# Down products of three feed-forward blocks with stationary weights over 512 tokens, copied by ScalarE and turned back behind the next middle product

## What is computed

```python
def _tlin(x, w, s):
    return jnp.einsum('bsi,oi->bso', x, w) * s
h = silu(_tlin(xn, w1_w, w1_s)) * _tlin(xn, w2_w, w2_s)     # 128 -> 512 features ("up")
h = gelu(_tlin(h, h1_w, h1_s))                              # 512 -> 512 (first middle product)
h = gelu(_tlin(h, h2_w, h2_s))                              # 512 -> 512 (second middle product)
ffn = _tlin(h, w3_w, w3_s)                                  # 512 -> 128 ("down")
# the state-space part: y of 256 features per token, gated, and then projected to 128
attn = residual + jnp.einsum('bli,di->bld', y * silu(z), out_proj_w)
x = x + attn + ffn                                          # both are added to the same rows
```

## Time and profile before

| what | value |
| --- | --- |
| median of three timed runs | 603.2 us (603.0 to 603.21) |
| the profiled execution, its own time | 603.02 us |
| span of its trace, first to last instruction | 600.9 us |
| mean granted TensorE clock | 0.994 |
| busy share of the span: PE, DVE, ACT, POOL | 94%, 66%, 78%, 20% |

### The profile page before, as it was taken

One profiled execution on the slowest core, in us unless ns is written; L12 is line 12 of the kernel. 1 busy time (PEld: TensorE's weight loads), 2 busy tenths in 40 slices (PEclk: granted clock), 3 DMA queues, 4 the chain that ended last, 5 costly groups with the idle time before them and its releaser, 6 DMA issues.

```text
span 600.9 us, 11244 instructions
## 1 busy us (share of the span) xinstructions
PE 562.0 (94%) x3944; PEld 330.8 (55%) x3944; DVE 399.1 (66%) x1060; ACT 470.0 (78%) x669; POOL 120.8 (20%) x161
## 2 busy tenths in 40 slices
PE   6899999999999999999887899698699999999998
PEld 3343434443443434333334587386478887887887
DVE  6784887666363453685527355887888788698773
ACT  5699999989899999999795366479598686685673
POOL 2063221120020030103601355112012010010010
PEclk9999999999999999999999999999999999999999
DMA  7212011024222210400317220200000000000000
GB/s 223 47 25 67 2 27 47 11 88 159 89 107 107 89 72 2 137 6 14 112 42 227 66 77 37 83 2 0 1 1 2 1 17 1 2 17 1 2 19 17
DMA packets 30982, 30.72 MB, mean 51 GB/s; under 512 B 6848, under 2 KB 20960, under 8 KB 30928
## 3 DMA queue, kind: packets, MB, share of 16 engines
q1 hardware_dynamic: 29680, 27.45, 14.6%
q0 software_dynamic: 1248, 2.57, 1.2%
HBM read 13.44 MB, written 12.89 MB: 44 GB/s over the span
## 4 chain that ended last, share of the span: by engine, by line
PE 70%; DVE 15%; ACT 7%; issue 6%; DMA 1%; POOL 0%; DVEq 0%; ACTq 0%; another core or an unknown queue 0%; POOLq 0%
PE ps L1414 18%; PE ps L1393 9%; PE ps L92 6%; PE ps L94 6%; PE ps L93 5%; ACT r L1002 3%; PE ps L1725 2%; PE ps L1494 2%; PE ps L1600 1%; PE ps L1307 1%; PE ps L1763 1%; PE ps L1766 1%; PE ps L1486 1%; PE ps L1730 1%; PE ps L1267 1%
## 5 line engine op out<-in xcount | busy, mean ns | idle before, releaser
L1002 ACT ACTIVATE r<-ps 128x1024 f32<-128x1024 f32 x272 | 257.5, 1041 | 19.6 <-PE ps L1393 17.0
L1414 PE MATMUL ps<-r 128*32 128x512 f32 (+3 forms) x1280 | 144.8, 539 | 0.9 <-DVE r L2185 0.5
L858 POOL TENSOR_SCALAR_AFFINE_SELECT r<-r 128x512 f32<-128x512 f32 (+1 forms) x80 | 47.0, 589 | 206.0 <-ACT r L1002 205.7
L1393 PE MATMUL ps<-r2r 32*128 32x512 f32 (+3 forms) x640 | 80.2, 445 | 4.2 <-ACT r L1002 2.5
L1393 PEld LDWEIGHTS ps<-r2r 32*128 32x128 f32 x640 | 35.6, 182 | 46.9 <-ACT r L1002 21.3
L901 POOL TENSOR_TENSOR r<-r 128x512 f32<-128x512 f32 x16 | 22.6, 1414 | 151.0 <-ACT r L1210 130.1
L1414 PEld LDWEIGHTS ps<-r 128*32 128x32 f32 x1280 | 27.7, 108 | 40.5 <-issue 27.3
L94 PE MATMUL ps<-r2r 128*128 128x512 f32 (+1 forms) x104 | 39.0, 375 | 0.0
L1279 PE MATMUL ps<-consts 128*128 128x512 bf16 x98 | 25.4, 400 | 8.4 <-DMA consts<-in_consts 4.4
L93 PE MATMUL ps<-r2r 128*128 128x512 f32 (+1 forms) x88 | 32.7, 372 | 0.0
L876 POOL DMA_INDIRECT rows_by_token<-r x23 | 23.6, 1025 | 23.8 <-ACT r L1065 14.1
(11 more groups left out here) (436 smaller groups left out, 1206.6 us busy)
## 6 DMA issues: line engine op xcount, KB each, us to landing
rows_by_expert<-r SPq DMA_DIRECT2D x34, 258.0 KB, 2.5
r2r<-r2r SPq DMA_DIRECT2D x56, 64.0 KB, 2.0
r<-in_f_W SPq DMA_DIRECT2D x1, 2048.0 KB, 9.4
r<-rows_by_expert SPq DMA_DIRECT2D x23, 64.5 KB, 1.8
res<-in_x SPq DMA_DIRECT2D x4, 256.0 KB, 4.0
r<-in_g_h1T SPq DMA_DIRECT2D x1, 1024.0 KB
r<-in_g_h2T SPq DMA_DIRECT2D x1, 1024.0 KB
r<-rows_by_token SPq DMA_DIRECT2D x4, 256.0 KB, 4.0
```

What stands on the lines that cost most here:

```text
L858: pool.affine_select(blk, blk, pattern, ALU.is_ge, nothing, base=0, channel_multiplier=-1).then_inc(s_msk, 1)
L1002: act.activation(probs[:, n % PBUFS, :, :], ps[:, b:b + 2, :], ACT.Exp).then_inc(s_exp, 1)
L1393: m = pe.matmul(ps[:, 2 * (n % SBUFS) + h, at:at + TB - query], kst[32 * j:32 * j + 32, group, P * kt:P * kt + P], qst[32 * j:32 * j + 32, ...
L1414: m = pe.matmul(ps[32 * j:32 * j + 32, 6, query:TB], vp[:, kt, group, :], probs[:, (2 * v + j // 2) % PBUFS, j % 2, at:at + TB - query], s ...
```

## The change

`down(b)` of blocks 0 to 2 swaps the operands. The weights `f3[:, k, :]` are now stationary and the activations `fc[k]` of all 512 tokens move: four matmuls of 512 columns, and two of 384 columns with the projection weights `owT` stationary for the first three tiles. The result has features on partitions. ScalarE copies it into SBUF (`down_copied`, in slot 0 of the next block, ahead of its first Gelu). TensorE turns it back with four 128x128 transposes (`turned_back`) behind the first middle product of the next block, into a PSUM bank that it now takes in the round as a unit "BACK". VectorE's `down_added(b - 1)` moves from the end of slot 0 to slot 2, between `state_carried` and `last_chunk_added`. Block 3 keeps the old form under the name `last_down`.

What waited for `s_f4` because the activations or `yg` were still being read waits for the new `s_fdt` (the new down product) instead. The middle product that reuses the bank of the down product waits for the copy (`s_fdc`), and the first of the second middle products waits for `down_added` through the bank of the turned result. To free two semaphores, two counters are merged into others, `s_skt` into `s_kt` and `s_pace` into `s_msk`; the same instructions wait for the same events.

```diff
+        down_features = xn_flat[:, TB:2 * TB]
...
         for b in range(NB):
-            FFN_PE += [("MID1", b, o) for o in range(FO)]
+            for o in range(FO):
+                FFN_PE += [("MID1", b, o)] + ([("BACK", b - 1, 0)] if b and not o else [])
...
             def last_gelu(b, o):
                 act.wait_ge(s_f3, FO * b + o + 1)
                 if b:
-                    act.wait_ge(s_f4, b)
+                    act.wait_ge(s_fdt, b)
...
+            def down_copied(b):
+                act.wait_ge(s_fdt, b + 1)
+                act.activation(down_features, ps[:, ffn_bank("DOWN", b, 0), :], ACT.Copy).then_inc(s_fdc, 1)
...
                         gated_high(b, FO - 1)
                         if not b:
                             decays(0)
+                        else:
+                            down_copied(b - 1)
                     middle_gelu(b, o)
...
             def down(b):
                 bank_free(("DOWN", b, 0))
+                own = TPB - 1
+                for k in range(FO):
+                    pe.wait_ge(s_fg3, FO * b + k + 1)
+                    pe.matmul(ps[:, ffn_bank("DOWN", b, 0), :], f3[:, k, :], fc[k], start=(k == 0), stop=False)
+                pe.wait_ge(s_cg, TPB * b + own)
+                for m_ in range(MI):
+                    m = pe.matmul(ps[:, ffn_bank("DOWN", b, 0), 0:P * own].rearrange("p (n t) -> p n t", n=own),
+                                  owT[:, m_, :], yg[:, 0:own, m_, :], start=False, stop=(m_ == MI - 1))
+                m.then_inc(s_fdt, 1)
+
+            def turned_back(b):
+                bank_free(("BACK", b, 0))
+                pe.wait_ge(s_fdc, b + 1)
+                for i in range(TPB):
+                    m = pe.transpose(ps[:, ffn_bank("BACK", b, 0), P * i:P * i + P], down_features[:, P * i:P * i + P],
+                                     ident)
+                m.then_inc(s_f4, 1)
...
                 for o in range(FO):
                     middle(b, o)
+                    if b and not o:
+                        turned_back(b - 1)
...
-                down(b)
+                if b < NB - 1:
+                    down(b)
+                else:
+                    last_down(b)
...
                         state_carried(s // 2 - 1)
                         if o == 2 and b:
+                            down_added(b - 1)
                             last_chunk_added(b - 1)
                             finished(b - 1)
                         weighted(s // 2)
-                        if o == 0:
-                            down_added(b - 1)
```

More of the change, by code:

```diff
@@ L386, in build @@
         s_ksplit = sem("key_splits_ready")
-        s_kt = sem("first_keys_and_queries_transposed")
+        s_kt = sem("first_keys_and_queries_turned_and_spread")
         s_kc = sem("transposed_keys_copied")
         s_sqc = sem("first_query_stacks_copied")
-        s_skt = sem("first_key_stacks_spread")
         s_skc = sem("first_key_stacks_copied_by_act")
@@ L397, in build @@
         s_vws = sem("summary_values_compact")
-        s_msk = sem("diagonals_masked")
+        s_msk = sem("diagonals_masked_then_late_rows_moved")
         s_og = sem("gated")
@@ L429, in build @@
         s_scat = sem("rows_scattered")
-        s_pace = sem("rows_moved_by_gpsimd")
         s_hs = [sem(f"slot_rows_loaded{g}") for g in range(NG)]
@@ L492, in build @@
         s_f4 = sem("ffn_down_products")
+        s_fdt = sem("ffn_down_features")
+        s_fdc = sem("ffn_down_features_copied")
         s_fr = sem("ffn_scaled")
@@ L870, in _ @@
                 rows_scattered(i)
-                pool.sem_inc(s_pace, 1)
+                pool.sem_inc(s_msk, 1)
             for t in range(SLOTS):
@@ L960, in _ @@
             act.activation(keysT, ps[:, 4, :], ACT.Copy).then_inc(s_kc, 1)
-            act.wait_ge(s_skt, 1)
+            act.wait_ge(s_kt, 2)
             act.activation(kst[:, 0, 0:TB], ps[:, 1, :], ACT.Copy).then_inc(s_skc, 1)
@@ L1004, in _ @@
                 if k == 0:
-                    act.wait_ge(s_skt, 2)
+                    act.wait_ge(s_kt, 4)
                     act.activation(kst[:, 1, 0:TB], ps[:, 6, :], ACT.Copy).then_inc(s_skc, 1)
@@ L1363, in _ @@
             pe.wait_ge(s_xnTc, 2)
-            keys_stacked(1, 0).then_inc(s_skt, 1)
+            keys_stacked(1, 0).then_inc(s_kt, 1)
             pe.wait_ge(s_split, 1)
@@ L1374, in _ @@
                     elif k == 1:
-                        keys_stacked(6, 1).then_inc(s_skt, 1)
+                        keys_stacked(6, 1).then_inc(s_kt, 1)
                     elif k == of_round(1, 0)[0]:
@@ L1564, in _ @@
             for i in range(TPB):
-                pe.wait_ge(s_pace, i + 1)
+                pe.wait_ge(s_msk, 2 * len(DIAG) + i + 1)
                 kept_busy(1, 2)
@@ L1632, in bank_free @@
                         pe.wait_ge(s_fg3, FO * b + o + 1)
+                    elif what == "DOWN":
+                        pe.wait_ge(s_fdc, b + 1)
                     else:
@@ L1718, in down, with last_down @@
                 bank_free(("DOWN", b, 0))
+                own = TPB - 1
[9 more added lines that the diff above has]
+                bank_free(("BACK", b, 0))
+                pe.wait_ge(s_fdc, b + 1)
+                for i in range(TPB):
+                    m = pe.transpose(ps[:, ffn_bank("BACK", b, 0), P * i:P * i + P], down_features[:, P * i:P * i + P],
+                                     ident)
+                m.then_inc(s_f4, 1)
+            def last_down(b):
+                bank_free(("DOWN", b, 0))
                 pe.wait_ge(s_fg3, FO * (b + 1))
                 for i in range(TPB):
-                    own = i < TPB - 1 or b == NB - 1
                     final = TPB * b + i == NCH - 1
@@ L1724, in down @@
                     for k in range(FO):
[L1725 to L1730, removed]
+                        pe.matmul(dst, fc[k][:, P * i:P * i + P], f3[:, k, :], start=(k == 0), stop=False)
+                    pe.wait_ge(s_cg, TPB * b + i + 1)
+                    for m_ in range(MI):
+                        m = pe.matmul(dst, yg[:, i, m_, :], owT[:, m_, :], start=False, stop=(m_ == MI - 1))
                     if TPB * b + i == NCH - 2:
@@ L1950, in _ @@
             split(0)
-            dve.wait_ge(s_kt, 2)
+            dve.wait_ge(s_kt, 3)
             dve.tensor_copy(qst[:, 0, 0:TB], ps[:, 0, :]).then_inc(s_sqc, 1)
@@ L2665, in state_carried @@
                 if i >= TPB:
-                    dve.wait_ge(s_f4, i // TPB)
+                    dve.wait_ge(s_fdt, i // TPB)
                     if n == TPB - 1:
@@ L2687, in down_added @@
                 dve.wait_ge(s_f4, b + 1)
-                n = TPB if b < NB - 1 else TPB - 1
+                what, n = ("BACK", TPB) if b < NB - 1 else ("DOWN", TPB - 1)
                 blk = res[:, TPB * b:TPB * b + n, :]
-                dve.tensor_tensor(blk, blk, ps[:, ffn_bank("DOWN", b, 0), 0:D * n].rearrange("p (i d) -> p i d", i=n),
+                dve.tensor_tensor(blk, blk, ps[:, ffn_bank(what, b, 0), 0:D * n].rearrange("p (i d) -> p i d", i=n),
                                   ALU.add).then_inc(s_fr, 1)
```

## The result

The changed kernel takes 604.95 us (median of 8 runs, 604.25 to 606.71); the kernel before, on the same chip, 603.21 us (8 runs, 601.35 to 604.11). The ratio is 1.0037, with a 95% interval of 1.0022 to 1.0052, so the change costs about 2.2 us. The forecast was 605.5 us.

A forecast was written before the change was run, and what follows sets the result against it. TensorE was taken as the bound, except VectorE in slots 1 to 4 of blocks 1 and 2. 3 x 0.34 + 2 x 0.72 = 2.46 us on 603.02 gave 605.5 us, range 604.6 to 606.6, for 8 in 10 603.6 to 606.9.

The forecast's parts named there:

- The bounds: Last stage: TensorE sets the pace, except in slots 1 to 4 of blocks 1 and 2, where VectorE does.
- The down product: On TensorE, the swapped product takes 4.84 us instead of 4.91 per transition; about 0.1 us saved.
- The rival that long products are much faster: 512-column instructions of the down product take 0.23 us, giving 599.3 us; chance 0.05.
- the ratio of 1.6: Down product: a 512-column matmul costs 1.6 times a 128-column one; the kernel would come out near 597 us.
- The transposes: Four new transposes on TensorE in a stretch without gaps add 0.44 us per transition, hidden by nothing.
- TensorE's share: Down product and transposes together cost TensorE 0.34 us in each of three transitions, 1.02 us in all.
- The addition: `down_added` moved into slot 2 on VectorE costs 0.72 us in each of blocks 1 and 2, 1.44 in all.
- The rival that it is absorbed: The addition in slot 2 finds slack on VectorE, only TensorE's term is left: 604.0 us; chance 0.16.
- The taps: VectorE's taps beside GpSimd's multiplication: another tap meets it, cost 0, range 0.4 us less to 0.2 more per block.
- The copy: ScalarE's copy out of PSUM, ahead of the first Gelu, takes 0.66 us and costs 0.
- the dear reading of line 1506: Down product at 0.56 us per 512-column instruction, +1.3 us per transition; part of a costs-more rival, 606.9 us and more, chance 0.13.

The follow-up runs named there:

- the short multiplication: Changed kernel with GpSimd's multiplication cut to one of four parts: 602.35 us, ratio 0.9993, stage 127.30 us.
- the early tap: Kernel before, with the first tap of slot 1 in blocks 1 and 2 put ahead of `chunk_started`: 602.29 us, ratio 0.9978, stage 126.81 us.
- the first two experiments: Changed kernel with `down_added` in slot 1: 604.73 us, ratio 1.0023; changed kernel with `down_added` of blocks 0 to 2 left out: 604.66 us, ratio 1.0009.
- the changed kernel with slot 1 and the tap: Changed kernel with `down_added` in slot 1 and the first tap of blocks 1 and 2 behind it, both ahead of `chunk_started`: 602.77 us, ratio 1.001.

## Why the prediction was right, point by point

**The bounds.** That VectorE sets the pace from `chunk_started` to `up_gated` in blocks 1 and 2, and TensorE everywhere else, fits every run; where an edit took enough off VectorE's stretch (the short multiplication, the early tap), TensorE's waits vanished. The addition, with the tap that it moved, cost 1.7 us in slot 2 (130.48 - 128.74) and 0.1 in slot 1 (128.86 - 128.74); the doubled transposes cost the same 0.43 in block 3 as in the others.

**The down product.** Forecast 4.84 us, measured 4.72, a saving of 0.19 instead of 0.1. The price of 0.44 us per 512 columns, read from line 1329, was a little high: it is 0.429, and 0.322 for 384 columns. One instruction of 512 columns costs 3.9 times one of 128 (0.111), so what is saved is 0.015 us for each four that become one. The rival that long products are much faster needed less than 0.34 us and falls. So does the ratio of 1.6 that the prediction took from the Trainium skill, page "TensorE: Matmul & The Clock Gate", section "Back-to-back issue gap": it isn't borne out for these 32-bit values.

**The transposes.** Forecast 0.44 us, measured 0.44, and nothing hides them (0.43 each time when doubled). TensorE's share is therefore 3 x 0.25 = 0.75 us and not 1.02.

**The addition.** Forecast 0.72 us in each of two blocks, measured 0.71. The rival that it is absorbed falls with the first two experiments, which take 1.6 and 1.7 us off the stage by moving it or leaving it out. As predicted, TensorE waits at `state` (0.60 us, forecast 0.7) and still at the up product (0.5, forecast 0.4), and neither in block 3.

**The taps.** Here a term was mis-sized: forecast 0, with 0.2 as its upper end, measured 0.14 per block. That the collision moves to the first tap was right; that one instruction pays in either case was right too, but not that it pays the same: the first tap took 1.79 us where the second had taken 1.67. Three taps took 3.29 us, not 3.15 (the forecast named 3.2). Nor did GpSimd follow VectorE by 0.4 us. It starts 11.84 us after `chunk_started` of slot 1 (495.45 - 483.61), before 11.77 (493.86 - 482.09), so by 0.07. The move of the addition back into slot 1 undoes this as well.

**The copy.** Forecast 0. The copy took 0.60 us, and 0.89 us of waiting is left behind it (forecast about 0.5). No run took it out by itself, but little is left for it: the changed kernel with slot 1 and the tap is 0.78 us behind the kernel before with the tap, where three times 0.25 us is TensorE's share.

**The sum.** 0.75 + 2 x (0.71 + 0.14) = 2.45 us, measured 2.43 on the stage, forecast 2.46. The two errors, 0.27 too much on TensorE and 0.28 too little on VectorE's taps, cancelled; that the sum comes within 0.03 us is luck, since either error alone would have put it nearly 0.3 us off. On the time, 603.02 + 2.46 gave 605.5; the median is 604.95. The difference of the two medians, 1.74 us, the ratio's 2.2 and the stage's 2.43 agree as far as executions that differ by 2.5 us among themselves allow. Executions at a granted clock of 1.0 overlap less: 604.25, 604.67 and 604.97 us with the change, and 601.37 to 602.4 us (median of 13: 601.81) for the kernel before in the later runs.

**A rival's size.** The prediction let the dear reading of line 1506 add 1.4 us, for one transition. A price of 0.56 us per instruction would have held in all three and added 4.2. With 0.429 measured it makes no difference to the outcome.

## What to carry to other kernels

Before moving an instruction, look up in the chain which engine sets the pace at the place it leaves and at the place it enters: the same 0.68 us cost nothing in a slot where its engine waits, and its full length, twice, where the others wait for it. Swapping the operands so that fewer, longer matmuls do the same columns saves little where time follows the columns, and whatever turns the result back has to be paid out of that. A wait that shows up ahead of a bound stretch is the place to put work in: one tap in each of two blocks moved there gained 1.24 us, more than the 0.75 that the whole rewrite cost on TensorE. And beside GpSimd's multiplication belongs an instruction that reads PSUM, such as the addition itself; the next section has the rows for this, but no run tried it.

## What the runs showed of the hardware

A VectorE instruction that starts while GpSimd multiplies is held up if both its tensor inputs are in SBUF. With 512 columns it ends 0.55 us after GpSimd does, whether it is the second tap, the first tap (495.69 to 497.48, GpSimd until 496.94), or `middle_low` (487.19 to 488.97, GpSimd until 488.42), which alone takes 0.69 us. With 256 columns (in block 3 of the kernel before, line 2678 at 580.54 us, 1.36 us long instead of 0.42) it ends 0.28 us after. An instruction that reads PSUM keeps its length, as `up_gated` in the kernel before, which ends before GpSimd does:

```profile
504.73 1.42 POOL L901 TENSOR_TENSOR r<-r 128x512 f32<-128x512 f32 x1 [9.38 <-ACT r L1210]
504.91 0.68 DVE L2567 SCALAR_TENSOR_TENSOR r<-r,ps 128x512 f32<-128x512 f32 x1
```

All overlaps of the last stage in the traces with the full multiplication go this way. The other direction shows too: GpSimd takes 1.27 to 1.30 us where it starts beside no VectorE instruction with two SBUF inputs, and 1.38 to 1.73 us where it starts in the middle of one. With a quarter of the multiplication three taps fall from 3.3 to 2.40 us. The Trainium skill, page "SBUF — State Buffer", section "SBUF: two separate sides", says that a VectorE instruction with two SBUF inputs and a GpSimd instruction that reads SBUF share a port, and that the one that starts first holds it for its whole length; by that rule, the trace agrees, and the price here is about 1 us for each multiplication that a VectorE instruction of 512 columns runs into.

A wait that belongs to the Gelu can stand ahead of ScalarE's table load, and hold up the load as well. The load of 1.28 us was hidden as long as the wait for the product stayed with the Gelu. With one more wait at the Gelu it was not, and the Gelu came 1.30 us after the product instead of right behind it, though nothing of the load itself was changed.

Executions of one kernel differ by more than most edits here are worth, and with the mean granted clock: the kernel before took 601.37 to 602.4 us in executions with a clock of 1.0 and 606.97 in one with 0.983. The changed kernel's profiled execution reached `down(0)` 1.29 us later than that of the kernel before; over all traces this start lies between 469.99 and 472.98 us, whichever kernel the run was made from, so it says nothing of the change. The length of one stage in the trace told edits of 0.3 to 0.4 us apart, and blocks 1 and 2 of one trace agree within 0.02 us; the medians did not tell them apart.
